# Expert chunks of layer 0 loaded in pairs: 1 MB a transfer instead of 512 KB, into the same ring of four places

## The reference, cut to what matters

```python
hr = jnp.square(jax.nn.relu(jnp.einsum('nc,ech->enh', flat_h, K_rwkv)))   # K_rwkv (2, 256, 1024)
out_rwkv = jnp.einsum('enh,ehc->enc', hr, V_rwkv)                         # V_rwkv (2, 1024, 256)
out_trans = flat_h @ W1 * jax.nn.sigmoid(flat_state @ W2) @ W3
all_out = jnp.concatenate([out_rwkv, out_trans[None]], axis=0)
onehot = jax.nn.one_hot(flat_w, E, dtype=flat_h.dtype)
final = jnp.einsum('ne,enc->nc', onehot, all_out) * scale
```

## Time and profile before

| | us |
|---|---|
| median of 3 runs | 1795.3 |
| lowest and highest | 1792.99, 1796.29 |
| the profiled execution | 1809.51 |
| its span, first to last instruction | 1807.8 |
| TensorE busy in the span | 1471.5 |
| VectorE, ScalarE, GpSimd busy | 1144.7, 975.0, 344.8 |

### The profile page before, as it was taken

One profiled execution on the slowest core, in us unless ns is written; L12 is line 12 of the kernel. 1 busy time (PEld: TensorE's weight loads), 2 busy tenths in 40 slices (PEclk: granted clock), 3 DMA queues, 4 the chain that ended last, 5 costly groups with the idle time before them and its releaser, 6 DMA issues. The chain is left out here.

```text
span 1807.8 us, 27211 instructions
## 1 busy us (share of the span) xinstructions
PE 1471.5 (81%) x8399; PEld 1147.0 (63%) x8441; DVE 1144.7 (63%) x2967; ACT 975.0 (54%) x1484; POOL 344.8 (19%) x311
## 2 busy tenths in 40 slices
PE   5734667999899999999999987771886977999996
PEld 1223556788778777787877876661554325787875
DVE  4643444567566756676667653331788986888985
ACT  2212214555665566455655564452895815878783
POOL 1100101110122012210221011005540012343430
PEclk9656677989899989998999999895898989999998
DMA  6840102433444334433543345653220001111111
GB/s 178 286 118 17 40 12 87 135 125 114 145 152 139 123 124 157 144 133 115 167 133 128 122 140 176 196 178 122 79 78 8 0 15 33 59 59 58 58 59 36
DMA packets 115172, 192.01 MB, mean 106 GB/s; under 512 B 18033, under 2 KB 84145, under 8 KB 115058
## 3 DMA queue, kind: packets, MB, share of 16 engines
q1 hardware_dynamic: 96256, 145.64, 25.7%
q0 software_dynamic: 13664, 43.28, 6.8%
q10 hardware_dynamic: 5170, 2.10, 0.6%
HBM read 134.08 MB, written 57.97 MB: 106 GB/s over the span
## 5 line engine op out<-in xcount | busy, mean ns | idle before, releaser
L899 ACT ACTIVATE hr_r<-pair 128x512 f32<-128x512 f32 x136 | 79.9, 588 | 159.5 <-PE pair L158 159.1
L156 PE MATMUL pair<-kv_ring,hr_lo 128*128 128x256 f32 x544 | 158.5, 291 | 3.9 <-DVE acc_s L1364 3.9
L157 PE MATMUL pair<-kv_ring,hr_hi 128*128 128x256 f32 x544 | 155.1, 285 | 0.0
L158 PE MATMUL pair<-kv_ring,hr_hi 128*128 128x256 f32 x544 | 155.0, 285 | 0.0
L1955 POOL DMA_INDIRECT ff<-x_scratch,slots x64 | 89.0, 1391 | 241.5 <-POOLq L1434 140.5
L156 PE MATMUL pair<-th_hi,kv_ring 128*128 128x512 f32 x272 | 114.4, 420 | 24.1 <-issue 15.6
L1357 DVE TENSOR_TENSOR hr_lo<-hr_sq,hr_hi 128x512 fp32r<-128x512 f32 x136 | 94.0, 692 | 53.1 <-ACT hr_sq L913 25.6
L1975 ACT ACTIVATE ff<-pair,hbs,s1h 128x512 f32<-128x512 f32 x128 | 95.5, 773 | 55.5 <-PE pair L2045 50.0
L762 POOL TENSOR_TENSOR rs<-var,neg_half 128x8 f32<-128x8 f32 x16 | 32.1, 2003 | 441.1 <-DVE var L1213 441.1
L156 PEld LDWEIGHTS pair<-kv_ring,hr_lo 128*128 128x128 f32 x544 | 105.8, 195 | 12.7 <-issue 9.4
L157 PE MATMUL pair<-th_lo,kv_ring 128*128 128x512 f32 x272 | 108.4, 399 | 0.0
(11 more groups left out here) (389 smaller groups left out, 4334.0 us busy)
## 6 DMA issues: line engine op xcount, KB each, us to landing
kv_ring<-expert_scratch SPq DMA_DIRECT2D x136, 512.0 KB, 3.7
acc_s<-rows_scratch SPq DMA_DIRECT2D x17, 528.0 KB, 5.2
xn_s<-rows_scratch SPq DMA_DIRECT2D x17, 512.0 KB, 3.9
x_scratch<-acc_s SPq DMA_DIRECT2D x17, 512.0 KB, 5.2
text_scratch<-text SPq DMA_DIRECT2D x17, 512.0 KB, 3.9
expert_scratch<-expert_space POOLq DMA_DIRECT2D x2, 4096.0 KB, 21.2
x_in<-in_x SPq DMA_DIRECT2D x16, 512.0 KB
out<-ff SPq DMA_DIRECT2D x16, 512.0 KB, 2.9
```

The costliest lines, as they stand in the source:

```text
L156: pe.matmul(dst, st[1], mv[0], start=start, stop=False, skip_group_check=True)
L157: pe.matmul(dst, st[0], mv[1], start=False, stop=False, skip_group_check=True)
L158: return pe.matmul(dst, st[0], mv[0], start=False, stop=stop, skip_group_check=True)
L899: s.activation(hr_r[:, c % 2, :], up_ps[:, (c % 2) * T:(c % 2 + 1) * T], ACT.Relu).then_inc(relu_done, 1)
```

## The change

A transfer now carries chunks c and c+1 (c even) into the neighbouring places c % 4 and c % 4 + 1. It waits for one more down product, since both places must be free, and it raises only the semaphore of the even chunk. up(c) of an odd chunk waits for the semaphore of the even one. In SyncE's order the entries of the odd chunks are gone: chunk 5 comes with 4, 7 with 6 (now ahead of load_x), 1 with 0 (now ahead of store_x3 and load_small), 3 with 2 (now ahead of load_sums). The ring, the places, the order of TensorE, VectorE, ScalarE and GpSimd and all the arithmetic are as before.

```diff
--- before.py
+++ after.py
@@ -709,9 +709,10 @@
                             if t == 0 and c == 0:
                                 sp.wait_ge(exp_stored, 32)
                             sp.wait_ge(routed, t + 1)
-                            after(sp, down_done, HC * t + c - 3)
+                            after(sp, down_done, HC * t + c - 2)
                             e = sp.value_load(tile_ex[0:1, t:t + 1], min_val=0, max_val=1)
-                            sp.dma_start(kv[:, c % RING, :].bitcast(F32), exp_dram[bass.ds(e * HC + c, 1)].rearrange("o p n -> (o p) n")).then_inc(kv_loaded[c], 16)
+                            sp.dma_start(kv[:, c % RING:c % RING + 2, :].bitcast(F32),
+                                         exp_dram[bass.ds(e * HC + c, 2)].rearrange("o p n -> p o n")).then_inc(kv_loaded[c], 16)
                         return piece
 
                     def store_x3(t):
@@ -725,18 +726,14 @@
                     def iteration(i):
                         tile(i, 5, store_text)
                         tile(i, 3, load_expert(4))
-                        tile(i, 3, load_expert(5))
                         tile(i, 3, load_expert(6))
                         batch(i, 0, load_x)
-                        tile(i, 3, load_expert(7))
                         tile(i, 2, load_rows)
                         tile(i, 2, load_expert(0))
                         tile(i, 4, store_x3)
                         batch(i, 0, load_small)
-                        tile(i, 2, load_expert(1))
                         tile(i, 2, load_expert(2))
                         tile(i, 3, load_sums)
-                        tile(i, 2, load_expert(3))
                     for i in range(NTILE + 1 + FAR):
                         iteration(i)
                     sp.wait_ge(x3_stored, 16 * NTILE)
@@ -1098,7 +1095,7 @@
                     def up(c):
                         def piece(t):
                             pe.wait_ge(th_lo_done, t + 1)
-                            pe.wait_ge(kv_loaded[c], 16 * t + 16)
+                            pe.wait_ge(kv_loaded[c - c % 2], 16 * t + 16)
                             after(pe, relu_done, HC * t + c - 1)
                             for k in range(KC):
                                 st = (kv[:, c % RING, k * P:(k + 1) * P], kv[:, c % RING, 512 + k * P:512 + (k + 1) * P])
```

## The result

| | before | pairs |
|---|---|---|
| median, us | 1795.8 (4 runs) | 2098.5 (4 runs) |
| lowest and highest | 1792.99, 1803.93 | 2095.23, 2102.66 |
| the profiled execution | 1809.51 | 2102.66 |
| its span | 1807.8 | 2099.8 |

The ratio is 1.168 (95% interval 1.164 to 1.172): the change costs 303 us. The forecast was 2096.

A forecast was written before the change was run, and what follows sets the result against it. TensorE's own queue was taken as the path in the loop, so added waits are paid nearly in full: 213 us idle plus 88 us clock, 301 in all, gave 2096 us on the median; range 2005 to 2175.

The forecast's parts named there:

- Chunks 2 and 3: Before up(2), directly behind down(7), nothing covers the pair's 6.5 us latency: +6.7 us, tiles 1 to 12, 80 us.
- Chunks 4 and 5: Before up(4), 4.0 us of work behind down(1) covers part of the 6.5 us latency: +2.5 us, 13 times, 33 us.
- Chunks 6 and 7: Before up(6) and up(7), pair released by down(3): +2.8 us net of the old wait, 13 times, 36 us.
- (b): Rival: pairs land slowly, up to 7.4 us, and the sums behind them hold collect and h_low: 2214 us, chance 0.14.
- Chunks 0 and 1: Before up(0), 6.6 us of work behind down(5) just covers the pair: 0, up to +1.8 us a tile.
- SyncE's queue: Loads and stores behind the pairs on SyncE, the sums among them, go later but are covered in full turns: 0.
- Clock: TensorE's granted clock falls behind the three waits: 3.5+0.8+2.0 us a turn, with the last tiles 88 us, bounds 0 and 130.
- Last tiles: Tiles 14 to 16 lack front work as cover, 16.7 us each; with tile 13 and others 64 us idle, 10 clock.
- The total: Whole kernel: 213 us idle plus 88 us clock, 301 us more, 2096 us on the median; chance 0.62.
- (a): Rival: the waits come but TensorE's clock holds, stalls only moving an existing low stretch: 2008 us, chance 0.15.
- (c): Rival: not slower; larger transfers remove the waits before up(7), 1.9 us in the loop: 1793 us, chance 0.03.
- (d): Rival: the pair for chunks 2 and 3 is released by down(6), so 80+42 us go: 1974 us, chance 0.06.

The follow-up runs named there:

- e2: The pairs kernel with only chunks 2 and 3 loaded singly again, with the waits and places of the kernel before: 1933.5 us, ratio 1.076.
- e7: The pairs kernel with GpSimd's scatter of rows held back until VectorE's low half of the next batch is done: 2081.6 us, ratio 1.159.
- e5: The pairs kernel with the load of the sums put ahead of the pair 2 and 3 on SyncE: 2097.2 us, ratio 1.167.
- e4: The pairs kernel with products whose result nothing reads put on TensorE in the waits before up(2), up(4) and up(6): 2005.1 us, ratio 1.115.
- e6: The kernel before with a ring of eight places and single 512 KB chunks, each released a whole turn ahead: 1777.8 us, ratio 0.990.
- e1: The pairs kernel with a ring of eight places, each pair released a whole turn earlier: 1781.2 us, ratio 0.991 against the kernel before.

## Why the prediction was right, point by point

- **Chunks 2 and 3: +6.7 a turn, 12 times, 80.** Up(2) started 6.30 us behind down(7) in the mean of tiles 1 to 12, so +6.46 and 78. e2 shows it is this pair.
- **Chunks 4 and 5: +2.5, 33 in all.** Up(4) started 5.8 behind down(1) instead of 4.0: +1.8, and 13 times that is 24. My pair's latency of 6.5 was too long, since a pair lands in 5.1 us, below my lower bound of 5.3 and with it below the sum of 3.7 and 1.9.
- **Chunks 6 and 7: +2.8, 36 in all.** It was the other way: +3.6 us idle a turn (11.9 less 6.5 and 1.8), some 47. The step that failed is one latency for all pairs: up(6) started 7.3 us behind down(3), not 6.5, since this one runs into the scatter (e7), which I had only as a part of rival (b). The base was off too: I took up(7) to start 5.1 behind down(3) from one turn, where the mean of twelve is 4.8. The two errors, -9 and +11, cancel.
- **Chunks 0 and 1: 0.** Up(0) came 6.6 us behind down(5) as before.
- **SyncE's queue: 0.** Right in full turns: the sums were issued 2.3 us behind the end of down(7) (764.39), as I had reckoned, collect began 9.0 us behind it, I had 9.7, and the wait of h_low was covered. The total of e5 agrees, but as a sum of two small effects: up(2) 0.3 us later in each full turn, and in the last tiles down(0) 1.1 us earlier.
- **Clock: 3.5+0.8+2.0=6.3 us a turn.** Measured 6.4, and e4 gave back just that. That it comes from the waits is shown; how it splits over the three is shown for one: e2's 47 us of busy time in twelve turns is 3.9 a turn for the pair 2 and 3, where I had 3.5. My strict reading of the Trainium skill (TensorE: Matmul & The Clock Gate, "HAM oscillation — how this bites in real kernels": a wait for a DMA between bursts throttles the clock each time) gave an estimate of 130 for the whole; measured are 77 in the full turns and 26 behind them, 103, between that and my 88.
- **Last tiles: 64 idle, 10 clock.** Measured 46 and 26, together 72 against 74. I underrated the clock here: this stretch is 35% idle now, and its granted clock of 0.76 is the lowest. Down(0) started 10.5 us behind down(7) in tiles 14 to 16, not 11.6, for the sums landed sooner, and up(4) 5.8 behind down(1), not 6.5. The two errors also belong together: at 1.2 GHz the six products of up(2) take 2.6 us instead of 1.4, but inside the wait for the sums, so time that I had counted idle was busy at the low clock.
- **The total** is right to 0.1% in part by luck: four terms were off by 9, 11, 16 and 18 us, two to either side.
- **The rule on transfer size.** The Trainium skill's formula (DMA: Bandwidth & Descriptors, "Anatomy of one DMA — SWDGE (gpsimd) path") gives, as an estimate, 4.4 us for a pair; it is fitted for GpSimd's path. The measured landing on SyncE's is 5.1, and 4.8 at the least: between it and my 5.5. The Trainium skill's rule to batch to 1 MiB (same page, "Measured (HBM→SBUF, 128 partitions, SWDGE, issued from GpSimd)") brought nothing here (e6 against e1). That throughput wasn't short would explain it: the mean DMA share of a turn was 42%.
- **Rivals.** (a), the clock holds, is refuted by the 77 us of busy time and e4. (b), slow landings everywhere, is refuted by the median of 5.1. (c) and (d) are refuted by up(2)'s 6.3 us. (c)'s price of 1.9 us was too low as well: with the waits before up(7) gone, e1 and e6 are 16 and 19 us faster than the kernel before; in e1's twelve turns more of the gain is clock (8.6 us) than idle time (5.2).

## What to carry to other kernels

Count, for each buffer of a ring, what work lies between the event that frees it and its next reader, and compare that with issue plus landing; merging two transfers takes the later of the two releases for both, and where the reader follows the release directly the whole latency is paid in each turn (up(2): 6.3 us). If larger transfers are wanted, widen the ring by the same factor first; here twice the places was worth 0.9 to 1.0% with either size. And a wait on TensorE can cost more than its length: here 77 us of clock came with 142 us of idle time in the twelve turns (0.54), and 0.63 for each us of the wait before up(2) (e2).

## What the runs showed of the hardware

- A 1 MB load landed 5.1 us after its issue against 3.7 for 512 KB: 1.4 us more for the second 512 KB, less than the 1.9 that the 274 GB/s of the earlier trace rows give. Its issue took SyncE 0.39 us against 0.35.
- An indirect scatter under way at the same time made such a load longer: 5.9 to 6.5 us over twelve turns, against 4.8 to 5.1 with the scatter held back (e7).
- With the waits filled, TensorE's granted clock was 0.95 over twelve turns (e4), against 0.93 in the kernel before, though a turn still had 6.5 us idle and that of the kernel before 4.3; with the waits empty, 0.84.
